# First attention on one core: units of one key tile, two batches and half of their queries, with near products of double width and values two units behind

## The reference

```python
scores = jnp.einsum('bhid,bhjd->bhij', q, k) * scale + gated_bias
attn = jax.nn.softmax(scores, axis=-1)
out = jnp.einsum('bhij,bhjd->bhid', attn, v)
```

## Time and profile before

| | us |
|---|---|
| median of the runs | 2298.37 |
| the profiled execution | 2297.82 |
| its span, first to last instruction | 2296.0 |
| busy: TensorE products | 2004.4 |
| busy: VectorE | 1625.2 |
| busy: ScalarE | 1348.2 |
| busy: POOL | 1099.2 |

### The profile page before, as it was taken

One profiled execution on the slowest core, in us unless ns is written; L12 is line 12 of the kernel. 1 busy time (PEld: TensorE's weight loads), 2 busy tenths in 40 slices (PEclk: granted clock), 3 DMA queues, 4 the chain that ended last, 5 costly groups with the idle time before them and its releaser, 6 DMA issues. The chain is left out here.

```text
span 2296.0 us, 56479 instructions
## 1 busy us (share of the span) xinstructions
PE 2004.4 (87%) x17787; PEld 1018.4 (44%) x17787; DVE 1625.2 (71%) x3441; ACT 1348.2 (59%) x2150; POOL 1099.2 (48%) x987
## 2 busy tenths in 40 slices
PE   5569999999999999975799759999999999998576
PEld 3324444444444444444344214444444444444355
DVE  4778888888888888767565776666666666664696
ACT  2226666666666666542455437777777777777121
POOL 1132322232223222414355317877877787877464
PEclk8869999999999999986899979999999999999787
DMA  5521111122112211100000460011111011100000
GB/s 133 156 62 51 55 54 49 50 55 53 49 50 55 53 49 51 47 11 1 1 1 0 154 194 29 29 41 28 41 28 42 28 42 28 42 14 1 0 14 23
DMA packets 127050, 107.03 MB, mean 47 GB/s; under 512 B 39636, under 2 KB 102724, under 8 KB 126956
## 3 DMA queue, kind: packets, MB, share of 16 engines
q1 hardware_dynamic: 124640, 103.37, 16.5%
q10 hardware_dynamic: 2316, 2.64, 0.4%
HBM read 76.01 MB, written 29.53 MB: 46 GB/s over the span
## 5 line engine op out<-in xcount | busy, mean ns | idle before, releaser
L1048 DVE TENSOR_REDUCE b_mx<-psum 128x1 f32<-128x512 f32 x1024 | 663.8, 686 | 145.7 <-PE psum L867 82.6
L1032 ACT ACTIVATE b_prob<-psum 128x1024 f32<-128x1024 f32 x512 | 524.3, 1024 | 319.8 <-PE psum L899 319.7
L1806 POOL TENSOR_TENSOR f_plo<-f_prob,f_phi 128x512 f16<-128x512 f32 x512 | 587.6, 1158 | 169.4 <-ACT f_phi L1931 144.2
L1949 DVE TENSOR_REDUCE f_mx<-psum 128x1 f32<-128x512 f32 x512 | 328.7, 683 | 169.0 <-PE psum L1826 167.9
L1930 ACT ACTIVATE f_prob<-psum 128x512 f32<-128x512 f32 x512 | 308.1, 602 | 158.1 <-PE psum L1837 153.4
L947 PE MATMUL psum<-b_prob,b_v 128*32 128x256 f32 x4096 | 328.3, 392 | 1.6 <-ACT b_prob L1032 0.5
L1931 ACT ACTIVATE f_phi<-psum 128x512 f16<-128x512 f32 x512 | 306.4, 598 | 0.0
L805 POOL COPY b_v<-v 128x64 f32 x64 | 15.2, 238 | 596.1 <-PE psum L947 595.8
L899 PE MATMUL psum<-b_diag,b_toep 128*128 128x79 f16 (+1 forms) x4224 | 267.4, 208 | 0.0
L899 PEld LDWEIGHTS psum<-b_diag,b_toep 128*128 128x128 f16 x4224 | 235.9, 99 | 9.1 <-issue 2.6
L808 POOL TENSOR_TENSOR b_diag<-flip,grev 128x1024 f16<-128x1024 f16 x128 | 239.8, 1895 | 0.0
(11 more groups left out here) (312 smaller groups left out, 3407.4 us busy)
## 6 DMA issues: line engine op xcount, KB each, us to landing
d_qk<-e_qk SPq DMA_DIRECT2D x64, 256.0 KB, 2.6
b_toep<-d_line SPq DMA_DIRECT2D x128, 64.0 KB
f_qa<-d_qk SPq DMA_DIRECT2D x64, 128.0 KB, 2.8
f_ka<-d_qk SPq DMA_DIRECT2D x64, 128.0 KB, 2.9
b_q<-d_q SPq DMA_DIRECT2D x128, 54.0 KB
d_k<-a_qk SPq DMA_DIRECT2D x48, 128.0 KB, 2.3
b_toep<-d_line SPq DMA_DIRECT2D x128, 32.0 KB
b_q<-b_m SPq DMA_DIRECT2D x256, 1.0 KB
```

What stands on the lines that cost most here:

```text
L1032: nc.scalar.activation(prob[:, t % 4, :].rearrange("p (a n) -> p a n", a=2), ps[:, EXP + 2 * (t % 2):EXP + 2 * (t % 2) + 2, :], ACT.Exp).t ...
L1048: nc.vector.tensor_reduce(mx[:, b, t, half:half + 1], ps[:, bank, :], AX.X, ALU.max).then_inc(s.max_read, 1)
L1806: nc.gpsimd.tensor_tensor(plo[:, t % 4, at], prob[:, t % 4, at], phi[:, t % 4, at], ALU.subtract).then_inc(s.plo_ready, 1)
L1949: nc.vector.tensor_reduce(mx[:, b, t, half:half + 1], ps[:, MAX + half, :], AX.X, ALU.max).then_inc(s.max_read, 1)
```

## The change

A unit is now a key tile of two batches and half of their queries. An item is a head, a pair of batches and one of two query halves (`idx` = 2 x pair + half): the first half has query tiles 0, 1, 4, 5, the second 2, 3, 6, 7. A unit's two banks hold 256 queries of either batch. Far products are 256 columns wide per batch and group, those of the second batch behind the far ones of the maxima. One near product serves both batches, so it is 158 or 256 wide, and only key tiles next to the item's queries have them: `ORDER` gives the order of key tiles. In the first half positions 0, 2, 4 and 6 have two query tiles near (256 and 158 columns), positions 1, 3 and 5 one (158), position 7 none; in the second half positions 0, 2, 4 and 6 have two, 3, 5 and 7 one and 1 none. Values are multiplied two units behind, the outputs are turned after unit 3 and divided at unit 4, by two multiplies. The maxima's 16 rows go to four places in either batch, by eight stores of two rows. Loads are split into those for the maxima and those for the exponentials, per pair; POOL makes the diagonals for the maxima in a buffer of their own. Semaphores of the phase before are cleared at the start.

```diff
+        LAG = 2
+        QUARTER = N // 4
+        ORDER = ((0, 2, 1, 3, 4, 6, 5, 7), (2, 0, 3, 1, 6, 4, 7, 5))
...
-        toep = sb("b_toep", [P, SLOTS, 2, 3 * P], F16)
-        diag = sb("b_diag", [P, SLOTS, 2, TB, P], F16)
+        toep_max = sb("b_toep_max", [P, 2, 3 * P], F16)
+        toep_exp = sb("b_toep_exp", [P, 2, 2, 3 * P], F16)
+        diag_max = g.combT[:, :].rearrange("p (s t e) -> p s t e", s=SLOTS, t=TB)
+        diag_exp = g.x16[:, :, :].rearrange("p a t -> p (a t)").rearrange("p (s x t e) -> p s x t e", s=SLOTS, x=2, t=TB)
...
-        OUT_STEP, M_STEP = 2, 4
+        OUT_STEP, M_STEP = 3, 4
...
-        LOADS = 16
+        MAX_LOADS, EXP_LOADS, M_STORES = (8, 6), 16, 8
+
+        def query_tile(idx, n):
+
+            bb, i, y = n // 4, n // 2 % 2, n % 2
+            return 2 * (idx // 2) + bb, 4 * i + 2 * (idx % 2) + y
...
+                def load_max(h, pair):
+
+                    for half in range(2):
+                        sp.wait_ge(s.max_psum[half], done(TB * (4 * (h - 1) + 2 * pair + 1) + TB - 1))
                     head = bass.ds(h, 1)
-                    j = loaded[b]
-                    one = lambda ap: ap.rearrange("a p n -> (a p) n")
-                    for half in range(2):
-                        mine, tok = slice(half * BANK, (half + 1) * BANK), bass.ds(b * N, N)
-                        part = bass.ds(b * N + half * BANK, BANK)
-                        for_exp, for_max = half * GROUP, (2 + half) * GROUP
-                        sp.dma_start(qs[b][for_max:for_max + M_ROW, :], one(g.d_q[head, :, tok])).then_inc(j, 16)
-                        sp.dma_start(qs[b][for_exp:for_exp + M_ROW, mine], one(g.d_q[head, :, part])).then_inc(j, 16)
-                        for side in range(2):
-                            sp.dma_start(ks[b][side][for_max:for_max + M_ROW, mine], one(g.d_k[side, head, :, part])).then_inc(j, 16)
-                            sp.dma_start(ks[b][side][for_exp:for_exp + M_ROW, :], one(g.d_k[side, head, :, tok])).then_inc(j, 16)
+                    for bb in range(2):
+                        b = 2 * pair + bb
+                        j = max_loaded[b]
+                        for half in range(2):
+                            mine, tok = slice(half * BANK, (half + 1) * BANK), bass.ds(b * N, N)
+                            part = bass.ds(b * N + half * BANK, BANK)
+                            rows = slice((2 + half) * GROUP, (2 + half) * GROUP + M_ROW)
+                            sp.dma_start(qs[b][rows, :], one(g.d_q[head, :, tok])).then_inc(j, 16)
+                            for side in range(2):
+                                sp.dma_start(ks[b][side][rows, mine], one(g.d_k[side, head, :, part])).then_inc(j, 16)
...
+                def load_exp(h, pair):
+
+                    for i in range(2):
+                        sp.wait_ge(s.exp_psum[i], done(TB * (4 * (h - 1) + 2 * pair + 1) + TB - 1))
+                    head = bass.ds(h, 1)
+                    j = exp_loaded[pair]
+                    for bb in range(2):
+                        b = 2 * pair + bb
...
-                def store_m(h, b):
-                    item = 4 * h + b
+                        sp.dma_start(toep_exp[:, pair, part, 0:2 * P], hankel(line, 0, 2 * P)).then_inc(j, 16)
+                        sp.dma_start(toep_exp[:, pair, part, 2 * P:3 * P], hankel(line, LINE_R, P)).then_inc(j, 16)
+
+                def store_m(h, idx):
+                    item = 4 * h + idx
                     sp.wait_ge(s.m_moved, done(item))
-                    for half in range(2):
-                        for part in range(2):
-                            row, at = half * GROUP + M_ROW + part, (2 * half + part) * (TB // 2)
-                            sp.dma_start(qs[b][row:row + 1, half * BANK:(half + 1) * BANK].rearrange("a (t p) -> a t p", p=P),
-                                         m16[at:at + TB // 2, b % 2, :]).then_inc(m_stored[b], 16)
-
-                for b in range(B):
-                    sp.sem_inc(m_stored[b], 64)
-                    sp.wait_ge(s.zeroed, b + 1)
-                    load(0, b)
+                    for bb in range(2):
+                        for i in range(2):
+                            for part in range(2):
+                                row, at = i * GROUP + M_ROW + part, 8 * bb + 4 * part + 2 * i
+                                q0 = i * BANK + (idx % 2) * QUARTER
+                                sp.dma_start(qs[2 * (idx // 2) + bb][row:row + 1, q0:q0 + QUARTER].rearrange("a (t p) -> a t p", p=P),
+                                             m16[at:at + 2, idx % 2, :]).then_inc(m_stored[idx], 16)
...
                 with sp.Fori(0, H0 - 1) as k:
-                    for b in range(B):
-                        store_m(k + (b + 1) // 4, (b + 1) % 4)
-                        load(k + 1, b)
-                for b in range(1, B):
-                    store_m(H0 - 1, b)
+                    load_exp(k, 1)
+                    store_m(k, 1)
+                    load_max(k + 1, 0)
+                    store_m(k, 2)
+                    load_exp(k + 1, 0)
+                    store_m(k, 3)
+                    load_max(k + 1, 1)
+                    store_m(k + 1, 0)
...
+                def for_max(h, pair):
+                    for half in range(2):
+                        pool.wait_ge(s.max_psum[half], done(TB * (4 * (h - 1) + 2 * pair + 1) + TB - 1))
+                    for b in (2 * pair, 2 * pair + 1):
+                        nc.gpsimd.tensor_tensor(diag_max[:, b, :, :], flips, gates(h, b, 0), ALU.mult).then_inc(s.diag_max_ready, 1)
+
+                def for_exp(h, pair):
+                    pool.wait_ge(s.av_ready, done(TB * (4 * (h - 1) + 2 * pair + 1) + TB - 1))
+                    for b in (2 * pair, 2 * pair + 1):
+                        nc.gpsimd.tensor_copy(vs[:, b, :, 0:D0], g.v[:, b * TB:(b + 1) * TB, bass.ds(h * D0, D0)])
+                        for part in range(2):
+                            ins = nc.gpsimd.tensor_tensor(diag_exp[:, b, part, :, :], flips, gates(h, b, part), ALU.mult)
+                    ins.then_inc(s.v_diag_ready, 1)
...
+                    return [x for x in near if x[1] // 2 == 2 * i + hf]
+
+                def exp_far(bb, i, idx, pos, left):
...
+                    opens = bb == 0 and not (left and c0 < mid < c1)
+                    at = bb * QUARTER - c0
+                    return nc.tensor.matmul(ps[:, bank, at + x:at + y], ks[b][int(not left)][rows, t * P:(t + 1) * P], qs[b][rows, x:y],
+                                            start=opens, stop=not exp_near_of(t, i, hf), skip_group_check=True)
...
+                            at = qt % 2 * P
+                            last = nc.tensor.matmul(both[:, :, at + x:at + y], toep_exp[:, pair, tp, blk * P:(blk + 1) * P],
+                                                    diag_exp[:, 2 * pair:2 * pair + 2, dp, qt, x:y],
                                                     start=False, stop=(tp, dp) == (1, 0), skip_group_check=True)
...
+                        pe.wait_ge(m_stored[idx], 16 * M_STORES * (h + 2))
...
+                    last = [None, None]
                     for left in (False, True):
+                        for i in range(2):
+                            last[i] = exp_far(0, i, idx, pos, left) or last[i]
+                    if ahead:
+                        at = [ring.index((pos, half)) for half in range(2)]
                         for half in range(2):
-                            last = exp_far(b, t, half, left) or last
+                            bank_free(h, idx, at[half])
+                        fars = max_fars(im, nm, [RING + x % BANKS for x in at])
+                    for left in (False, True):
+                        for i in range(2):
+                            last[i] = exp_far(1, i, idx, pos, left) or last[i]
                     if ahead:
-                        at = [ring.index((t, half)) for half in range(2)]
-                        for half in range(2):
-                            bank_free(h, b, at[half])
-                        maxima(bm, tm, [RING + x % BANKS for x in at])
-                    for half in range(2):
-                        last = exp_near(b, t, half) or last
-                    last.then_inc(s.exp_psum, 1)
-
-                def values(h, b, t):
-
-                    item = 4 * h + b
-                    tile = TB * item + t
-                    if t == 0:
+                        max_nears(im, nm, [RING + x % BANKS for x in at], fars)
+                    for i in range(2):
+                        (exp_near(i, idx, pos) or last[i]).then_inc(s.exp_psum[i], 1)
...
+                        last = nc.tensor.matmul(ps[32 * c:32 * c + VW, AV, 0:2 * P], vs[:, 2 * (idx // 2) + c % 2, ORDER[idx % 2][pos], :],
+                                                prob[:, pos % 4, c * 2 * P:(c + 1) * 2 * P],
```

(64 more changed lines are left out.)

102 lines of the change are left out of this document (55 added, 47 removed).

## The result

The changed kernel takes 2493.64 us, the median of four runs (2486.92 to 2496.62); the kernel before took 2300.18 beside it. The ratio is 1.0809, with an interval of 1.0731 to 1.0888: slower by some 193 us, where 73 were forecast and the range ended at 2412.

What follows compares the result with a forecast made beforehand. TensorE's stream was taken to bound the kernel, with a new wait for eight stores: 63 passages x 1.16 us = +73 on 2297.8 gave 2371 us. Forecast 2345 to 2400 (chance 0.66); 8 in 10 from 2288 to 2412.

Steps and rivals of the forecast that it cites:

- The view of what bounds the kernel: First attention: TensorE's stream bounds it, busy 96% at full clock; an item takes 13.49 us, about 1.2 of it waits.
- the slack of 1.1 us: Start of an item, kernel before: stores of the maxima release TensorE at 605.33, its far products start at 606.43.
- The stores: SyncE, maxima's rows: eight stores spaced 0.59 us instead of four make position 0 wait about 1.5 us per item.
- the rival that hides them: SyncE: two-row stores issue every 0.33 to 0.38 us, so no wait, period 13.1, 2273 us; chance 0.18.
- The item's period is 14.65 us, against 13.49: +1.16: Each item: position 0 begins at 9.60, then 5.05 us to position 3's maxima; 63 passages give +73 us.
- Without the wait 13.1 us: An item's period if TensorE didn't wait for the stores: 4.35 to position 5's maxima, then 8.77.
- Near products: TensorE's scores: 66 of double width instead of 132 per pair, bound by columns; saves about 0.08 us per item.
- Far products: TensorE: same 512 columns per row group in two pieces of 256; costs 0 to 0.03 us per unit, taken 0.01.
- third rival: TensorE's far products run in series, not beside the maxima's: 0.107 us per far group, +106, 2404 us; chance 0.07.
- Values two units behind: Exponentials get 0.57 us unneeded slack; outputs' turn one unit later is hidden in VectorE's stretch; net gain 0.2 us.
- POOL "cost 0": POOL multiplies three times per item instead of twice, 5.9 us of 13, due an item or more later; cost 0.
- Loads: SyncE: 60 loads per head instead of 64, each group over before the stores come up; cost 0.

Runs made afterwards that it cites:

- Experiment 3: The changed kernel with the maxima's rows reordered so that four stores of four rows do what eight did: 2305.44 us, ratio 1.0007 to the kernel before.
- experiment 2: The changed kernel with seven unused products of 512 columns ahead of TensorE's wait for the stores in each item: 2427.94 us, ratio 1.0542.
- experiment 11: The changed kernel, eight stores kept, with POOL's multiplies held back until VectorE's join of the maxima: 2485.85 us, ratio 1.0805.
- experiment 5: Experiment 3 with the outputs turned after unit 5 and divided at unit 6: 2323.72 us, ratio 1.0099.
- experiment 6: Experiment 3 with each near product of double width replaced by two of single width, same columns: 2403.31 us, ratio 1.0455.
- experiment 4: The changed kernel, eight stores kept, with values one unit behind and the outputs' turn and divide at their old places: 2552.28 us, ratio 1.1082.
- experiment 7: Experiment 3 with values one unit behind and the outputs turned after unit 2: 2484.58 us, ratio 1.0795.
- experiment 8: Experiment 7 with POOL's multiplies held back until VectorE's join of the maxima: 2336.73 us, ratio 1.0156.
- experiment 9: Experiment 3 with POOL's multiplies held back until VectorE's join of the maxima: 2295.71 us, ratio 0.9976.
- experiment 1: The kernel before with each of its four stores of the maxima cut into two of two rows: 2422.5 us, ratio 1.0519.

## Why the prediction was right in direction and wrong in size

**The view of what bounds the kernel** was right: the slack of 1.1 us in the earlier trace rows was the number on which the change turned. Experiment 3 shows it from the other side, as does the old kernel with eight stores.

**The stores.** Right as a mechanism: a wait in 63 items, and the rival that hides them is excluded by 0.56 us per issue and by the 109 us. Its terms were all somewhat low. From the read at unit 3 to the copied rows I had 3.81 us; the item at 698.84 has 3.99 (702.83), the one at 715.71 4.10 (719.81). In the first, the join ends 0.10 later than I had it (700.83), the divide 0.06 (702.11), and the rest lies in the turn and ScalarE's copy; in the second POOL holds the cast. From the first store to the release I had 4.13 + 1.64 = 5.77. It is 6.03 and 6.23: the spacing is (4.81 - 0.56) / 7 = 0.607 instead of 0.59, so the last store starts at 4.25, and from there it is 1.78 in the first case instead of 1.64. From position 0 to position 3's maxima I had 5.05; at full clock (experiment 2) it is 5.18 to 5.38 in four items in a row, 5.31 in the mean. In these items the three terms are 0.20, 0.24 and 0.26 too low, and an item is 15.36 long instead of 14.65. That is 63 x 0.7 = 44 us. Of the other 13 between 2371 and 2428, 9 stand behind the last copy of the maxima: from there to the end of the span it is 1307.7 us in experiment 2 (1118.88 to 2426.6) and 1298.7 before (997.29 to 2296.0). The sum had nothing there; 2 of them lie in the last item and 7 behind the stage; their cause stays open. The remaining 4 are in the passages at the two ends of the stage, which take up to 18.5 us.

**The step that failed** is the sentence "The item's period is 14.65 us, against 13.49: +1.16", and the sum made of it. It prices position 0 to position 3 behind a wait of 1.5 us with durations read in a stage without waits, at a clock of 1.00. Behind most of these waits the products of some 3.7 us ran at 0.55, or the clock fell a little later (0.54 to 0.76 over the 3.7 us). No row of before could give the size, nor in how many items the clock would fall. But the condition was there to be read: in the earlier trace rows the clock is 1.00 in a stage where TensorE is busy 96%, and I took every duration from it. A bound from the same rows would have been products at half clock from position 0 to position 3, 5.05 us more in an item, which reaches far past 2494 (2689). Experiment 2 gives this term 66 us.

The gap closes so: 73 forecast, 66 the clock, 44 the mis-sized terms (about 8 of these are POOL, experiment 11), 13 at the ends of the stage and behind it: 196, against 193 measured by the medians and 196 by the two profiled executions. More than half of the miss (66 of some 120) is thus the clock; the rest is the terms.

**Without the wait 13.1 us.** Wrong by 0.37: experiment 3 shows 13.47. TensorE waits for VectorE at the divide, at unit 4 and behind the empty position (0.33, 0.28 and 0.18 us), which is more than what is missing; but experiment 5 took the first of them away and gained nothing, so that these waits are the cause is argued, not shown. I had the uneven load in the sum, but not what it does to an engine that reads at an even pace. This term also carried the rivals: 2273 for hidden stores was out of reach, and so was the low end of the range.

**Near products.** 0.08 us for an item was about right (experiment 6, 0.03 to 0.05). The 0.035 us of a narrow product in the rows decided this, and the 81 ns of the Trainium skill (TensorE: Matmul & The Clock Gate, "Back-to-back issue gap") did not hold: by it, as an estimate, experiment 6 should have had some 2 us more in each item, not at each fourth. What the halved number is worth lies elsewhere, in the stalls at the loop's restart and the lower clock behind them, about 98 us between experiments 3 and 6. I had no row for that and no rival.

**Far products.** Right: no third rival. In the changed kernel's trace, where nothing waits, the second batch's pieces start 0.12 us behind the first's, beside the maxima's (700.12 and 700.24), and a far group takes 0.32 to 0.39 us.

**Values two units behind.** I called the further slack of no use. For ScalarE this holds. But the distance also sets when POOL starts. With one unit and the outputs' turn at its old place the kernel loses 59 us (experiment 4); at four stores the same edit leaves 189 us to the best kernel, and POOL's meeting with the join is 148 of them (experiments 7, 8 and 9). At eight stores this share was not measured.

**POOL "cost 0".** The cover that I named was one of deadlines: POOL is early enough. That it takes VectorE's time while it runs, I didn't ask. It is about 8 us here.

**Loads.** Cost 0 was right; none of them stands between two stores in the rows.

## What to carry to other kernels

An engine that now waits in each iteration doesn't only lose the wait: what it does next may run at half clock, in some iterations and not in others, so the sum needs durations at both levels, and a filler of unused products shows on the chip how much of a loss is clock. Before a step is cut finer, count the DMAs that the cut adds on the path: four added issues of 0.56 us outweighed everything that the new tiling could save. A background engine costs nothing only if it neither comes late nor runs beside small SBUF operations on the path; a wait that holds it back behind them was worth 8 to 148 us. Such a wait moves its later work as well, so look at what that work meets then.

## What the runs showed of the hardware

- TensorE's granted clock fell to 0.55 for 3.7 us behind a wait of 1.73 us, but stayed at 1.00 behind one of 1.82 us in the same kernel, behind seven of 14 waits of 1.44 us there, and behind those of 1.15 to 1.25 us in the middle of experiment 1.
- POOL's fp16 multiply of 1.89 us holds a cast and a subtraction of 8 columns on VectorE, which take 0.17 us alone, until it ends: 1.40 and 1.81 us in one join (experiment 4). Its operation of 8.67 us on 4480 columns holds such a subtraction for 8.51 us (experiment 9).
- TensorE stood still for 2.7 to 4.5 us at restarts of its loop, without any releaser in the profile, in the two kernels whose instruction queue moved 85 and 158 packets instead of 31; in the next 3.7 us the clock was 0.50 to 0.75.
